# A perceiver block on one core: rounds weighed in pairs, keys made in pairs between them, one exponential a round, and six rows of x kept

## The reference, cut to what matters

```python
x = x + _L0_xattn_ref(_layernorm(x), ctx, ...)   # a linear map, and the mean of the context
x = x + _L0_attn_ref(_layernorm(x), ...)         # self attention over 64 rows, 16 heads
x = x + _L0_ffn_ref(_layernorm(x), ...)          # shared part; 8 experts on all tokens' routing
x = x + _L1_xattn_ref(_layernorm(x), ctx, ...)   # 16 heads over 1601 keys: most of the work
x = x + _L1_attn_ref(_layernorm(x), ...)         # a convolution, a gated recurrence, a feed-forward part
x = x + _L1_ffn_ref(_layernorm(x), ...)          # 256 -> 1024 -> 256 with rounded activations
```

```python
k = split_heads(bank @ Wk.T + bk); v = split_heads(bank @ Wv.T + bv)
scores = einsum('bhqd,bhkd->bhqk', q / sqrt(16), k)
attn = softmax(scores, axis=-1)
ctx = einsum('bhqk,bhkd->bhqd', attn, v)
```

## Time and profile before

| what | value |
|---|---|
| median of 3 runs | 2220.2 us |
| the profiled execution's own time | 2225.24 us |
| its span | 2223.3 us |
| PE busy | 2024.7 us, 91% |
| DVE busy | 1353.2 us, 61% |
| ACT busy | 1092.5 us, 49% |
| POOL busy | 557.3 us, 25% |
| bytes moved | 243.94 MB, 110 GB/s |

### The profile page before, as it was taken

How to read it: one execution, slowest core, us unless ns; L and a number is a source line. 1 busy time by engine, 2 the same in 40 slices (tenths; PEclk the granted TensorE clock), 3 DMA queues, 4 the chain that set the end, 5 groups by cost and what they waited for, 6 DMA issues and landing times.

```text
span 2223.3 us, 73290 instructions
## 1 busy us (share of the span) xinstructions
PE 2024.7 (91%) x31814; PEld 1607.0 (72%) x31814; DVE 1353.2 (61%) x2525; ACT 1092.5 (49%) x2302; POOL 557.3 (25%) x966
## 2 busy tenths in 40 slices
PE   4788999899999999999999999999999988999977
PEld 4567777777878777777777778777777766777754
DVE  3456656755666666566666575675656566555543
ACT  2354555555455555445555544555544444444431
POOL 3122323222223131323223122322222222122201
PEclk8799999999999999999999999999999999999999
DMA  5343432343433333424232424143432302222121
GB/s 178 139 154 104 160 116 98 113 137 116 142 110 104 114 108 128 141 87 160 82 120 108 137 89 142 65 147 103 146 106 91 119 26 77 83 86 74 52 73 57
DMA packets 99116, 243.94 MB, mean 110 GB/s; under 512 B 13168, under 2 KB 19440, under 8 KB 98800
## 3 DMA queue, kind: packets, MB, share of 16 engines
q1 hardware_dynamic: 98800, 239.26, 31.8%
HBM read 235.94 MB, written 3.15 MB: 108 GB/s over the span
## 4 chain that ended last, share of the span: by engine, by line
PE 68%; DVE 14%; ACT 11%; issue 4%; SPq 1%; DMA 1%; POOL 1%; DVEq 0%; POOLq 0%; ACTq 0%
PE M L751 10%; PE M L758 9%; PE SC L930 9%; PE O L973 8%; PE SC L953 7%; ACT probT L1153 6%; DVE mx L1473 5%; PE X L780 4%; PE M L780 3%; PE SC L946 3%; PE X L1039 2%; PE M L821 2%; PE X L1027 1%; DVE V L1293 1%; ACT kT L1098 1%
## 5 line engine op out<-in xcount | busy, mean ns | idle before, releaser
L1473 DVE TENSOR_REDUCE mx<-SC 128x4 f32<-128x1600 f32 (+1 forms) x256 | 466.6, 1822 | 208.3 <-PE SC L930 204.6
L1153 ACT ACTIVATE probT<-SC 128x512 f32<-128x512 f32 (+1 forms) x1024 | 444.7, 522 | 168.0 <-PE SC L953 165.7
L1098 ACT ACTIVATE kT<-M,bk 128x400 f32<-128x400 f32 (+1 forms) x256 | 153.2, 598 | 536.4 <-PE M L751 536.0
L612 POOL TENSOR_TENSOR rowsT<-raw,rowsT 128x384 fp32r<-128x384 f32 (+1 forms) x256 | 280.7, 1117 | 403.5 <-ACT rowsT L1210 402.1
L758 PE MATMUL M<-wvs,rowsT 128*128 128x256 f32 x2496 | 361.2, 294 | 2.0 <-ACT kT L1098 1.6
L751 PE MATMUL M<-rowsT,wks 128*128 128x400 f32 (+1 forms) x1536 | 357.2, 368 | 3.5 <-POOL rowsT L612 2.3
L758 PEld LDWEIGHTS M<-wvs,rowsT 128*128 128x128 f32 x2496 | 316.3, 193 | 25.6 <-ACT kT L1098 2.0
L930 PE MATMUL SC<-kT,bdq 32*128 32x400 f32 (+1 forms) x2048 | 254.4, 566 | 71.7 <-ACT probT L1153 46.7
L751 PEld LDWEIGHTS M<-rowsT,wks 128*128 128x128 f32 x1536 | 271.9, 191 | 43.7 <-issue 22.3
L973 PEld LDWEIGHTS O<-probT,V 128*17 128x17 f32 x13312 | 197.2, 99 | 135.0 <-issue 120.2
L1293 DVE TENSOR_TENSOR V<-M,bv 128x256 f32<-128x256 f32 (+1 forms) x448 | 159.7, 398 | 205.9 <-PE M L758 197.5
(11 more groups left out here) (253 smaller groups left out, 2443.3 us busy)
## 6 DMA issues: line engine op xcount, KB each, us to landing
ring<-in_ws_dram SPq DMA_DIRECT2D x428, 256.0 KB, 4.6
raw<-in_ctx_dram SPq DMA_DIRECT2D x32, 1601.0 KB, 6.9
summed<-in_ctx_dram SPq DMA_DIRECT2D x60, 800.5 KB, 4.6
ring<-rounded_scratch SPq DMA_DIRECT2D x64, 256.0 KB, 6.0
out_dram<-x SPq DMA_DIRECT2D x16, 128.0 KB, 1.7
x<-in_x_dram SPq DMA_DIRECT2D x1, 1792.0 KB, 10.6
kT<-in_ctx_dram SPq DMA_DIRECT2D x2, 800.5 KB, 8.7
rounded_scratch<-wround SPq DMA_DIRECT2D x8, 128.0 KB, 2.1
```

Source lines behind the costliest of these rows:

```text
L612: pool.tensor_tensor(rowsT[1][:, c, at], raw[:, c, at], rowsT[0][:, c, at], ALU.subtract).then_inc(low_ready, 1)
L1098: act.activation(keys(n, c)[:, k0:k0 + kn], bank[:, 0:kn], ACT.Identity, bias=bk[:, c:c + 1]).then_inc(m_used[f % 2], 1)
L1153: act.activation(probT[step % 2][0:w, j, 0:len(ts), :].rearrange("p t q -> p (t q)"), SC[0:w, j, 0:len(ts) * P], ACT.Exp)\
L1473: dve.tensor_reduce(mx[c][:, :, n], SC[:, :, 0:KCH[n][1]], AX.X, ALU.max).then_inc(max_used, 1)
```

## The change

- `weigh` now takes a list of rounds. In slots 2, 4 and 6 it weighs the two rounds before, in slot 0 rounds 6 and 7 of the batch before, and in odd slots none. It never stands ahead of `maxima` now. The semaphore `weighed` counts pairs.
- `probT` has three buffers in place of two.
- A round's exponentials are one instruction over all four banks.
- `FIRST` and `SECOND` have a new order: keys in pairs behind `maxima` in slots 1, 5 and 7, one in slot 3, none in even slots; each slot has a value ahead of `maxima`, save slot 4, which has `key(0, 3)`; the single tile `value(6)` is in slot 2. `key(1, 3)` is made one slot earlier, in the batch before.
- The pieces of the split of `raw` are one slot earlier, and the third one waits for `value(4)` in place of `key(1, 3)`.
- `l0_s0` and `l0_s1` get a place of their own, "strips", between `maxima` and `weigh`.
- `x` has seven rows of tiles in place of 16: tile 0 keeps its own, the others share six. Six tiles are loaded at the start, and each further one when the tile that had its row is stored; SP waits for that store.

```diff
-L0_M = {..., (5, "second"): ["l0_s0", "l0_s1"], ...
+L0_M = {..., (5, "strips"): ["l0_s0", "l0_s1"], ...
...
-FIRST = [[value(4)], [value(5)], [value(0)], [value(6)], [value(1)], [key(0, 3)], [value(3)], []]
-SECOND = [[key(1, 3)], [key(0, 0)], [key(0, 1)], [key(0, 2)], [value(2)], [key(1, 0)], [key(1, 1)], [key(1, 2)]]
+FIRST = [[value(4)], [value(5)], [value(6)], [value(0)], [key(0, 3)], [value(1)], [value(3)], [value(2)]]
+SECOND = [[], [key(0, 0), key(0, 1)], [], [key(0, 2)], [], [key(1, 0), key(1, 1)], [], [key(1, 2), key(1, 3)]]
...
-PIECES = [(0, 4, key(1, 1)), (4, 7, key(1, 2)), (7, 10, key(1, 3)), (10, KT, value(VF - 1))]
+PIECES = [(0, 4, key(1, 1)), (4, 7, key(1, 2)), (7, 10, value(4)), (10, KT, value(VF - 1))]
...
-    for piece, at in enumerate((-1, 0, 1, 3)):
+    for piece, at in enumerate((-2, -1, 0, 2)):
...
+def rounds_weighed(b, k):
+    if k % 2:
+        return b, ()
+    return (b, (k - 2, k - 1)) if k else (b - 1, (STEPS - 2, STEPS - 1))
...
-        x = sp.sb("x", [P, NT, D])
+        x = sp.sb("x", [P, ROWS + 1, D])
...
-        probT = [sp.sb(f"probT{n}", [P, 4, 4, 2 * S]) for n in range(2)]
+        probT = [sp.sb(f"probT{n}", [P, 4, 4, 2 * S]) for n in range(3)]
...
                             store(t)
+                            if t + ROWS < NT - 1:
+                                sync.wait_ge(stored, 16 * (t + 1))
+                                sync.dma_start(x[:, ROW[TILE[t]], :], xs[:, TILE[t + ROWS], :]).then_inc(x_in, 16)
...
                     maxima(b, k)
+                    for what in pieces(b, k, "strips"):
+                        fill(what)
                     if k not in WEIGH_FIRST:
-                        weigh(*last(b, k))
+                        weigh(*rounds_weighed(b, k))
...
-                    for j in range(4):
-                        act.activation(probT[step % 2][0:w, j, 0:len(ts), :].rearrange("p t q -> p (t q)"), SC[0:w, j, 0:len(ts) * P], ACT.Exp)\
-                           .then_inc(exp_ready, 1)
+                    act.activation(probT[step % 3][0:w, :, 0:len(ts), :].rearrange("p j t q -> p j (t q)"), SC[0:w, :, 0:len(ts) * P], ACT.Exp)\
+                       .then_inc(exp_ready, 1)
```

More of the change, by code:

```diff
@@ L50 @@
 L0_TILE = [TILE[p] for p in L0_PLACE]
+ROWS = 6
+ROW = {tile: p % ROWS if tile else ROWS for p, tile in enumerate(TILE)}
 L0_START = [-22, -6, 7, 20, 33, 46] + [3 + 14 * n for n in range(4, NT - 2)]
@@ L71 @@
 L0_M = {(1, "second"): ["l0_turn1"], (2, "first"): ["l0_xa"], (3, "second"): ["l0_turn2"], (4, "first"): ["l0_qk"],
-        (4, "second"): ["l0_v"], (5, "second"): ["l0_s0", "l0_s1"], (8, "second"): ["l0_pt0"], (9, "first"): ["l0_pt1"],
+        (4, "second"): ["l0_v"], (5, "strips"): ["l0_s0", "l0_s1"], (8, "second"): ["l0_pt0"], (9, "first"): ["l0_pt1"],
         (9, "second"): ["l0_pv0"], (10, "first"): ["l0_pv1"], (10, "second"): ["l0_wo"], (12, "second"): ["l0_turn3"],
@@ L184, in pieces @@
 def pieces(b, k, half):
-    for what in (FIRST, SECOND)[half == "second"][k]:
+    for what in {"first": FIRST[k], "second": SECOND[k]}.get(half, ()):
         batch = b if what in OWN else b + 1
@@ L261, in count_all @@
                 count(what, XNUMBER, what[0], cycle)
-        for what in pieces(b, k, "second"):
-            count(what, NUMBER, what[1], cycle)
+        for half in ("strips", "second"):
+            for what in pieces(b, k, half):
+                count(what, NUMBER, what[1], cycle)
         for what in x_fills(b, k, "D"):
@@ L956, in scores, with weigh @@
                     mm.then_inc(score_filled, 1)
-                def weigh(b, k):
+                def weigh(b, rounds):
                     if not 0 <= b < B:
                         return
-                    c, g = k // NTG, k % NTG
-                    step = STEPS * b + k
-                    ts = list(tiles(g))
-                    if k == 0:
-                        pe.wait_ge(o_used, b + 1)
-                    if c == 0:
-                        wait_drained(pe, (b, "value", ts[-1] // 2, 0))
-                    pe.wait_ge(exp_ready, 4 * (step + 1))
-                    for n, t in enumerate(ts):
-                        w = held(t)
-                        for hh in range(8):
-                            col, og = hh % 4, 2 * c + hh // 4
-                            mm = pe.matmul(O[32 * col:32 * col + W1, og * S:(og + 1) * S], values(b, c)[0:w, t * 8 + hh, :],
-                                           probT[step % 2][0:w, hh // 2, n, (hh % 2) * S:(hh % 2 + 1) * S],
-                                           start=(k == 0 and n == 0 and hh < 4), stop=(t == KT - 1), skip_group_check=True)
-                    mm.then_inc(weighed, 1)
+                    for k in rounds:
+                        c, g = k // NTG, k % NTG
+                        step = STEPS * b + k
+                        ts = list(tiles(g))
+                        if k == 0:
+                            pe.wait_ge(o_used, b + 1)
+                        if c == 0:
+                            wait_drained(pe, (b, "value", ts[-1] // 2, 0))
+                        pe.wait_ge(exp_ready, step + 1)
+                        for n, t in enumerate(ts):
+                            w = held(t)
+                            for hh in range(8):
+                                col, og = hh % 4, 2 * c + hh // 4
+                                mm = pe.matmul(O[32 * col:32 * col + W1, og * S:(og + 1) * S], values(b, c)[0:w, t * 8 + hh, :],
+                                               probT[step % 3][0:w, hh // 2, n, (hh % 2) * S:(hh % 2 + 1) * S],
+                                               start=(k == 0 and n == 0 and hh < 4), stop=(t == KT - 1), skip_group_check=True)
+                    if rounds:
+                        mm.then_inc(weighed, 1)
                 def turn_rows(src):
@@ L1260, in _ @@
                         drain_x(what)
-                    for what in pieces(b, k, "second"):
-                        drain(what)
+                    for half in ("strips", "second"):
+                        for what in pieces(b, k, half):
+                            drain(what)
                     for what in x_fills(b, k, "D"):
```

56 lines of the change are left out of this document (28 added, 28 removed).

## The result

The changed kernel takes 2201.7 us, median of four runs (2193.6 to 2202.2), against 2220.3 us for the kernel before, measured beside it: ratio 0.9901, 95% interval 0.9888 to 0.9914. That is 18.6 us less, where 50 were forecast. The profiled execution took 2202.1 us (span 2200.3), 23 us less than that of before, and the rest of the accounting is made in it.

A forecast was written before the change was run, and what follows sets the result against it. PE's own work, then its waits for exponentials, reduce and late keys, was taken to bound the kernel. Terms summed to -50 us, from 2220.2 to a median of 2170 us (2150 to 2195, chance 0.60; wide range 2138 to 2209).

The forecast's parts named there:

- What bounds the kernel: PE's own work is the larger part; the rest is its waits, with gaps ahead of `scores` and `maxima` each slot.
- Crossings: Fewer changes between uses of PE's array, at 0.10 to 0.23 us each: -22 us, ends 0 and -40.
- The one exponential: On ACT, one instruction of 1.92 us for four of 2.06, in 80 gaps: -11 us, ends 0 and -20.
- Keys that came too late: `key(0, 3)` one slot earlier removes PE's 14.8 us wait ahead of `maxima`, part returning: -10 us, ends 0 and -14.8.
- Strips: PE's 8.5 us wait ahead of the strips goes, some waiting for DVE comes: -5 us, ends -8.5 and +5.
- Covers that change: Other PE work hiding the reduce and exponential shrinks in some slots, grows in others: +12 us, ends 0 and +35.
- ACT's order: First piece of the split runs in slot 6, where ACT has no key to move: -3 us.
- Clock: About half of the ten 1.2 GHz stretches behind strips stay: -12 us, ends +5 and -25.
- What costs nothing: Reloading rows of x makes SP wait for stores, hidden by the ring issued two slots ahead; 27 us if unhidden.
- A: Time saved on PE returns as gaps ahead of `scores` and `maxima`: -14 us, 2206 us; chance 0.24.
- B: The clock comes back wholly and the exponential gives 20 us: 2143 us; chance 0.11.
- C: 128 weighing matmuls behind a gap in slot 2 let the clock fall in all 31 batches: +49, 2269 us; chance 0.05.

The follow-up runs named there:

- a_weigh_each: Changed kernel with one round weighed in every slot, keys still in pairs: 2238.2 us, ratio 1.0085 to the kernel before.
- a_strip_second: Changed kernel with the strips of the first layer's scores back at the end of the slot's products: 2194.4 us, ratio 0.9889 to the kernel before.
- a_strip_dve: Changed kernel with DVE moving the strips right behind its reduce, ahead of the copy of O and the reciprocal: 2193.4 us, ratio 0.9881 to the kernel before.
- a_keys_single: Changed kernel with the key tables as before, one chunk a slot, and weighing still in pairs: 2247.4 us, ratio 1.0119 to the kernel before.
- a_no_soft: Changed kernel without DVE's normalisation of the first layer's softmax, so its result is wrong: 2185.6 us, ratio 0.9842 to the kernel before.
- a_tail: Changed kernel with the last batch's rounds weighed one in every slot: 2200.2 us, ratio 0.9905 to the kernel before.
- a_shift64: Changed kernel with 64 more small products on PE ahead of its first keys, shifting its later instructions: 2207.7 us, ratio 0.9939 to the kernel before.
- a_exp4: Changed kernel with four exponentials a round again in place of one: 2224.0 us, ratio 1.0017 to the kernel before.
- b_exp1_strips: Kernel before with one exponential a round and the strips behind `maxima`, no pairs: 2200.8 us, ratio 0.9916 to the kernel before.

## Why the prediction was wrong

- **What bounds the kernel** (PE's work, and two kinds of gap in a slot): right for `SC`, but it left out a third resource, the two M banks, which cost 27 us before already.
- **Crossings** (-22): right. PE's busy time fell by 33 us with 19 us less at 1.2 GHz, half of which is about 9; 24 remain. By `a_weigh_each` one crossing is nearer 0.08 us than 0.13, so part of the 24 may be other small savings. The far end of the term counted 178 crossings that go; in the traces PE changes between its three uses 1275 times before and 1105 after, which is 170.
- **The one exponential** (-11): right in kind and size; 1.88 us for 1.92 assumed, 9 us alone in the kernel before, 20 to 22 in the changed one, which is more than its term and its range had.
- **Keys that came too late** (-10): right or better. The wait is 0, and with the exponential the gaps ahead of `maxima` fell by 22 us for 21.
- **Strips** (-5): the two waits of the strips, for keys and for values, went (11.7 to 1.1 us), but a wait of values for DVE's move of the strips came (5.8 us, not in the forecast), and 1.7 more of the keys' (3 were forecast); and by `a_strip_second` the place is worth nothing here.
- **Covers that change** (+12): the failed step. It counted cover for `SC` alone and put the waits for the two M banks at nothing. For the reduce it was too dark (26.5 to 27.1 us, with 30 to 40 forecast). But it said that slots 1, 5 and 7 "have two keys, 2.4 us for 2.3, and hide late reduces better", and stopped there. The second key needs the bank that DVE has still to empty: M banks cost slot 1 13.5 us for 3.8 and slot 7 6.4 for 0.7. Slot 3, which has no pair, rose as much, from 1.2 to 13.7: there, among others, the values wait for the strips' move (5.8 us), a key for the same (1.8), and pieces of the first stages for DVE (2.9); `a_strip_dve` takes 8.4 us of it away. Over all slots M banks came to 19 us more, net of the 10.6 that the strips no longer wait; of the new waits 14.7 us are keys behind V. `a_weigh_each` and `a_keys_single` show that this wait hangs on what stands between value and second key, `a_no_soft` that it hangs on DVE's queue.
- **Not in the sum**: 9 us of waits for the instruction stream. They come with the 128 weighing products in a row: kernels with rounds in pairs have 7 to 11 us of them (6.6 in `a_tail`), those without at most 1.0. At one place it cost nothing and at another 4.1 us for 2.8 (under `a_shift64`), so the 9 us are their sum and not their price.
- **ACT's order** (-3): inside the gaps ahead of `maxima`, not told apart.
- **Clock** (-12): about -9. The premise was nearly right: nine of the ten falls behind strips follow a wait of the strips for ACT and one (18.4) a wait for DVE, but the strips of slots 6.3 and 22.0 had the same wait of 0.78 us and no fall. In the changed kernel four falls behind strips are left, 31 us for 58: in slot 3.1 as before but longer, new in 6.3, and in 13.3 and 20.3, where they come 7.3 us behind the strips' start and with the wait for DVE. The other seven are gone. New are falls behind long waits in slots 1.5, 3.3 and 5.1, and three in the last batch. Two stretches of the changed kernel, as in the earlier trace rows:

```profile
961.60:968.40 6.80, 5.21 (x23) 3.75 (x24) 3.29 (x7) 0.63 (x2) 1.38 (x2) 0.50 0.00 0
...
2094.90:2098.30 3.40, 3.40 (x35) 3.17 (x31) 2.03 (x5) 1.88 (x1) 1.73 (x5) 0.50 0.02 5
```

- **What costs nothing**: right. No wait of PE for the ring or for a row of x appears in the list; the stores took 2.8 us to landing for the 1.7 of the earlier trace rows.
- **Rivals**: the time is nearest to A (2206) and inside the wide range of 2138 to 2209, but that is luck: A's mechanism was gaps ahead of `scores` and `maxima`, and these fell by 21 us. B did not happen, nor C: 128 weighing products behind the exponential's wait drew no falls in the steady part.

What stays open: why single falls of the clock come in one execution and not in the next of the same kernel; and whether the keys' 14 us for V can be had back without giving up the pairs, as leaving out the softmax's end is no cure; and why the change without its exponential (`a_exp4`) loses 20 us and not the 15 of its profile.

## What to carry to other kernels

Count cover for each buffer that a moved piece touches, not only for the one whose wait you are removing: here two fills in a row needed both banks of a pair, and the engine that empties them was at times a slot behind. Changes that only work as a pair should be tried in all four combinations; here either pairing alone was slower than the kernel before, and the two small edits, one exponential and the strips' place, reached the time of the whole change without any pairs. Where a wait moves rather than goes, look first at the order inside the engine that releases it: DVE moving the strips before its sums was worth 4 to 10 us, beside 19 for the change.

## What the runs showed of the hardware

- **The instruction stream can stall TensorE.** The trace has 256 packets on the instruction queue, all of 16 KB, one in 8.4 us on average and 1.05 us long in the mean:

```profile
q8 instruction: 256, 4.19, 0.8%
```

  128 weighing products with their weight loads are 256 instructions in 1.98 us. In the changed kernel each of the nine waits with no releaser amid weighing or scores ended 1.3 to 1.5 us behind the end of such a packet. The Trainium skill (Runtime: NRT & Kernel Launch, Instruction fetch mechanics) says that an engine fetches blocks of 16 KiB, 256 instructions, by a queue of its own, and that this is mostly hidden. The packets' size agrees, and so does their number: PE's 31,814 matmuls and as many weight loads would fill 249 blocks of 256. Hidden it was in the kernel before (0.4 us), not where narrow products stand in long rows (9.4 us).
- **One ACT instruction may span four PSUM banks** and takes 1.88 us for 2048 elements a partition; four of 512 in a row take 2.06.
- **The clock fell** to 1.2 GHz where PE had waited: in the steady part of the changed kernel around waits of 2.77 us (203.9), 1.65 (316.5), 2.34 (432.6), 3.18 (961.6) and 2.62 (1415.6), and twice behind strips with waits of 0.5 to 1.8 us around them (299.4 and 514.5). Taking the wait away (slots 13.3 and 20.3 in `a_strip_dve`) took the fall away. A wait did not always bring one: in `b_exp1_strips` two waits of 3.32 us stand behind strips, and only the first has a fall.
